# Softplus steps, second norm, attention copies and jobs of the heads placed in other slots of a hand-ordered hybrid block

## The reference

```python
xn = (x - mu) * rsqrt(var + 1e-05) * ln_g + ln_b
dt_in, Bs, Cs = split(xn @ w_xproj)                    # 64, 64, 64 columns
delta = softplus(dt_in @ w_dt + b_dt)
h = exp(dt[:, :, None] * A) * h + (dt * xt)[:, :, None] * bt[:, None, :]   # for each token, h is 128 x 64
y = einsum('bdn,bn->bd', h, ct)
ssm_out = (y + x * D_ssm) @ w_ssm_out
attn = softmax(q k / sqrt(8) + bias, window of 96 keys for each 32 queries)   # 16 heads, 4 key heads
conv_out = silu(conv4(x) + b_conv)
mem_out = x @ w_wm + b_wm + 0.3 * softmax(x dec^T / sqrt(128)) @ dec
x1 = x0 + x + 0.2*attn @ wo + 0.45*ssm_out + 0.15*conv_out + 0.2*mem_out
out = x1 + layernorm(x1) @ int4(w) + bias + (layernorm(x1) @ a) @ b
```

## Time and profile before

| what | us |
|---|---|
| median of three runs | 1112.58 (1109.39 to 1113.99) |
| the profiled execution | 1114.23 |
| its span, first to last instruction | 1112.4 |
| busy in the span: DVE, POOL, ACT, PE | 979.3, 955.6, 837.5, 830.9 |
| front, until the first scan has ended | 39.9 |
| batch 0, from there to its last scan | 136.2 |
| batches 1 to 6, between their last scans | 132.1, 129.3, 133.4, 131.0, 132.1, 129.2 |
| batch 7 | 123.1 |
| after the last scan | 26.0 |

### The profile page before, as it was taken

How to read it: one execution, slowest core, us unless ns; L and a number is a source line. 1 busy time by engine, 2 the same in 40 slices (tenths; PEclk the granted TensorE clock), 3 DMA queues, 4 the chain that set the end, 5 groups by cost and what they waited for, 6 DMA issues and landing times. The chain is left out here.

```text
span 1112.4 us, 19145 instructions
## 1 busy us (share of the span) xinstructions
PE 830.9 (75%) x4151; PEld 339.3 (30%) x4151; DVE 979.3 (88%) x2299; ACT 837.5 (75%) x2255; POOL 955.6 (86%) x675
## 2 busy tenths in 40 slices
PE   5367878688777786877778777867868778677775
PEld 2023333233323332333323333323332333232332
DVE  2688999979997999979999699897999799999991
ACT  4468886788778878687877887679887887858871
POOL 6369988989898988988899898899989898979892
PEclk9556998978997989979898798888899798989897
DMA  5845667647675666666676476665666566766630
GB/s 111 196 126 169 180 159 185 171 138 198 163 183 155 185 167 159 172 157 172 168 203 161 128 191 162 167 173 159 177 176 183 153 187 165 188 161 164 196 95 9
DMA packets 124391, 181.18 MB, mean 163 GB/s; under 512 B 29263, under 2 KB 41056, under 8 KB 124256
## 3 DMA queue, kind: packets, MB, share of 16 engines
q1 hardware_dynamic: 123968, 179.56, 61.4%
q10 hardware_dynamic: 288, 0.20, 0.1%
HBM read 170.79 MB, written 5.05 MB: 158 GB/s over the span
## 5 line engine op out<-in xcount | busy, mean ns | idle before, releaser
L1389 POOL TENSOR_TENSOR prod<-hst,C 128x1024 f32<-128x1024 f32 x256 | 602.0, 2354 | 94.9 <-DVE hst L1201 94.4
L1201 DVE TENSOR_TENSOR_SCAN hst<-decay,bank 128x512 f32<-128x512 f32 x384 | 459.5, 1209 | 3.0 <-DVE cv_a L1236 2.8
L1189 DVE TENSOR_TENSOR bank<-bank,B 128x512 f32<-128x512 f32 x384 | 263.1, 685 | 52.6 <-PE bank L911 34.8
L665 ACT ACTIVATE decay<-wide,A_rep 128x512 f32<-128x512 f32 x384 | 273.4, 715 | 41.5 <-DVE hst L1201 31.2
L911 PE MATMUL bank<-spread,sel_bc 96*128 96x512 bf16 x384 | 164.5, 434 | 101.0 <-DVE hst L1201 90.6
L679 ACT ACTIVATE prob<-s_sb,nmax 128x96 f32<-128x96 f32 x512 | 185.2, 365 | 0.9 <-DVE nmax L1214 0.5
L1405 POOL TENSOR_TENSOR uwide<-uwide,B 128x512 f32<-128x512 f32 x128 | 162.7, 1271 | 22.5 <-DMA uwide<-u_rows 22.5
L935 PE MATMUL bank<-prod,sel_red 128*32 128x512 f32 x1024 | 164.9, 722 | 0.0
L1201 DVE TENSOR_TENSOR_SCAN hst<-bank,uwide 128x512 f32<-128x512 f32 x128 | 155.4, 1214 | 2.7 <-POOL uwide L1405 2.7
L951 PE MATMUL bank<-ident,prob 128*96 128x128 f32 x512 | 85.9, 295 | 77.5 <-ACT ao L695 58.3
L944 PE MATMUL bank<-k,q 128*128 128x384 f32 x256 | 126.7, 580 | 22.3 <-DVE nmax L1214 22.2
(11 more groups left out here) (189 smaller groups left out, 1027.4 us busy)
## 6 DMA issues: line engine op xcount, KB each, us to landing
wide<-dt_rows SPq DMA_DIRECT2D x512, 256.0 KB, 4.7
uwide<-u_rows SPq DMA_DIRECT2D x128, 256.0 KB, 4.1
spread<-parts SPq DMA_DIRECT2D x66, 32.0 KB, 4.1
x_sb<-in_L_attn_x_dram SPq DMA_DIRECT2D x8, 256.0 KB, 4.5
dt_rows<-sp_t SPq DMA_DIRECT2D x8, 256.0 KB, 2.6
out_dram<-outb SPq DMA_DIRECT2D x8, 256.0 KB, 3.9
vw<-v_tok SPq DMA_DIRECT2D x80, 16.0 KB, 3.3
u_rows<-uv SPq DMA_DIRECT2D x8, 64.0 KB, 2.4
```

The costliest lines, as they stand in the source:

```text
L665: nc.scalar.activation(to, wide[m % SLOTS][:, s % 2, :], ACT.Exp, scale=A_rep[:, g:g + 1]).then_inc(exp_done, 1)
L1189: v.tensor_tensor(uP[s % 4][:, :], uP[s % 4][:, :], B2[p][:, :], ALU.mult).then_inc(dbx_done, 1)
L1201: v.tensor_tensor_scan(hst[:, s % 8, :], kept, into[:, :], 0.0, ALU.mult, ALU.add).then_inc(scan_done, 1)
L1389: g.tensor_tensor(prod[:, 2 * (m % 4):2 * (m % 4) + 2, :], hst[:, 2 * (m % 4):2 * (m % 4) + 2, :], C2[p][:, :].unsqueeze(1).to_broadcast([ ...
```

## The change

Nothing is added to or taken from the arithmetic; steps change their slot, their place in a stream or, in the front, their engine.

1. **Softplus spread.** Exp moves from slot 20 to 24, adding 1 to slot 25 (`sum`), subtracting 1 to slot 26 (`less`), Ln from 21 to 28; POOL's four steps from 22-25 to 29-32, high, r, mid, lo from 28, 30, 33, 35 to 35, 37, 39, 41. SP's stores and part DMAs follow.
2. **Second norm.** residual, aggr2, root2, normalise2: 14, 16, 17, 20 to 16, 18, 19, 23. `zT` 23 to 26, `ffn` 25/26 to 28/29, output 29 to 31. `project` starts in slot 2, not 1.
3. **Jobs.** `B` and `C` from 34, 35 to 24, 25; xaT to v two slots later; `q` 60 to 59; `es0` 30 to 33, `conv` 40 to 38, `pt0` 37 to 46, `pt2`, `pt3` 57, 59 to 56, 57, `es1`, `es3` one slot earlier.
4. **Attention copy.** `ao_copy` of block k moves from the end of slot 6+3k+11 to the next slot, right behind `unit_exp`.
5. **Front.** DVE adds and subtracts 1 in one instruction beside ACT's Ln, which no longer waits for it; SP stores dt without waiting for u, and u after the first widening; ACT makes the first two exponentials ahead of the query copies, and the key copies in slot 1.
6. **Tail.** `proj` steps of the last batch in slots 58 to 61, six and seven ahead of the last reduction and eight and nine behind it; the bias matmul of the last `ffn` goes to the scores' free bank `sP` ahead of `zT`.

```diff
-JOB_AT = {13: ("t", "back"), 15: ("p", "xaT"), 17: ("p", "xnT"), 19: ("p", "dtpre"), 21: ("p", "v"),
-          23: ("t", "zT"), 26: ("t", "ffn"), 30: ("m", "es0"), 34: ("p", "B"), 35: ("p", "C"), 37: ("m", "pt0"),
+JOB_AT = {15: ("t", "back"), 17: ("p", "xaT"), 19: ("p", "xnT"), 21: ("p", "dtpre"), 23: ("p", "v"),
+          24: ("p", "B"), 25: ("p", "C"), 26: ("t", "zT"), 29: ("t", "ffn"), 33: ("m", "es0"),
...
-LAST_PROJECT = {60: (0, 1), 61: (2, 3), 62: (4, 5), 63: (6, 7)}
+LAST_PROJECT = {58: (0,), 59: (1,), 60: (2, 3), 61: (4, 5)}
...
-BIAS_LAG, EXP_LAG, INV_LAG, NORM_LAG, PT_LAG, PT_COPY_LAG, PV_LAG, AO_COPY_LAG = 2, (3, 4), 6, 5, 9, 9, 11, 11
+BIAS_LAG, EXP_LAG, INV_LAG, NORM_LAG, PT_LAG, PT_COPY_LAG, PV_LAG, AO_COPY_LAG = 2, (3, 4), 6, 5, 9, 9, 11, 12
...
             def softplus_exp(B):
                 wait(act, sp_step, B * N_SP + SP["relu"])
                 nc.scalar.activation(sp_e[:, :], sp_e[:, :], ACT.Exp, scale=-1.0).then_inc(sp_step, 1)
+
+            def softplus_sum(B):
                 wait(act, sp_step, B * N_SP + SP["exp"])
...
-                wait(act, sp_step, B * N_SP + SP["less"])
+                wait(act, sp_step, B * N_SP + SP["exp" if first(B) else "less"])
...
             def tail(B, p):
-                for n in range(8, N_PROJ - 1):
-                    project(B, p, n)
+                project(B, p, 6)
+                project(B, p, 7)
                 reduce_group(B, GROUPS - 1)
+                project(B, p, 8)
+                project(B, p, 9)
                 project(B, p, N_PROJ - 1)
                 tail_job("back", B, p)
+                wait(pe, s_max, NB * NBLK)
+                ffn_bias(sP)
                 tail_job("zT", B, p)
-                ffn_begin(B)
-                tail_job("ffn", B, p)
+                wait(pe, done["t"], job_count("t", B, "zT"))
+                ffn_half(0, sP)
+                filled(ffn_half(1, sP), "t", B, "ffn")
...
+                dve.wait_ge(sp_step, SP["exp"])
+                v.tensor_scalar(sp_t[:, :], sp_e[:, :], 1.0, 1.0, ALU.add, ALU.subtract).then_inc(sp_step, 2)
```

More of the change, by code:

```diff
@@ L648, in front @@
                             spread_parts(act, B, p, part)
+                        for s in range(AHEAD):
+                            unit_exp(B, s)
                         act.wait_ge(const_ready, 3)
                         act.wait_ge(head_tables, 3)
-                    if name == "k":
-                        for s in range(AHEAD):
-                            unit_exp(B, s)
-                    pre_job(name, B, p, front=True)
+                    if name != "k":
+                        pre_job(name, B, p, front=True)
             def unit_exp(B, s):
@@ L757, in body @@
                         unit_exp(B + 1, s + AHEAD - UNITS)
+                    k = block_at(s, AO_COPY_LAG)
+                    if k is not None:
+                        ao_copy(B, k)
                     if first(B):
+                        if s == 1:
+                            pre_job("k", B, p, front=True)
                         setup_step(s - SETUP_AT)
@@ L773, in body @@
                         probT_copy(B, k)
-                    k = block_at(s, AO_COPY_LAG)
-                    if k is not None:
-                        ao_copy(B, k)
                     t = memory_tile_at(s, M_EXP_LAG)
@@ L796, in body @@
                             softplus_exp(B + 1)
+                        if s == AT["sum"]:
+                            softplus_sum(B + 1)
+                        if s == AT["less"]:
+                            softplus_less(B + 1)
                         if s == AT["softplus_logs"]:
@@ L834, in setup_step @@
                     pe.wait_ge(w_in, 16 * N_W_DMA)
-                    wait(pe, done["p"], job_count("p", 0, "v"))
+                    wait(pe, done["p"], job_count("p", 0, "k"))
                     transposes([epi[:, c, :] for c in range(4)], CD, 128).then_inc(init, 1)
@@ L1004, in project, with ffn_half @@
                     filled(ins, "t", B, "proj")
-            def ffn_half(h):
+            def ffn_half(h, job=jobP):
                 for t in (2 * h, 2 * h + 1):
-                    ins = mm(jobP[:, t * D:(t + 1) * D], zT[:, t * 128:(t + 1) * 128], W2[:, :], start=False, stop=True,
+                    ins = mm(job[:, t * D:(t + 1) * D], zT[:, t * 128:(t + 1) * 128], W2[:, :], start=False, stop=True,
                              skip_group_check=True)
@@ L1014, in ffn_begin, with ffn_bias @@
                 fill("t", B, "ffn")
-                mm(jobP[:, :], ones_row[:, :], bias_row[:, :].unsqueeze(1).to_broadcast([1, NT, D]), start=True, stop=False,
+                ffn_bias(jobP)
+                ffn_half(0)
+            def ffn_bias(job):
+                mm(job[:, :], ones_row[:, :], bias_row[:, :].unsqueeze(1).to_broadcast([1, NT, D]), start=True, stop=False,
                    skip_group_check=True)
-                ffn_half(0)
             def tail_job(name, B, p):
@@ L1260, in output @@
                 wait_job(dve, "t", B, "ffn")
[L1261 removed]
+                v.tensor_tensor(outb[:, :, :], (sP if last(B) else jobP)[:, :].rearrange("p (t d) -> p t d", t=NT), x1[:, :, :], ALU.add) \
                     .then_inc(out_ready, 1)
```

32 lines of the change are left out of this document (18 added, 14 removed), and 4 rows, old and new, of the table JOB_AT.

## The result

The changed kernel takes 1164.47 us (median of 4 runs, 1159.72 to 1168.39), the kernel before 1112.65 beside it (4 runs). The ratio is 1.0468, 95% interval 1.0423 to 1.0514. The forecast was 1070, with a range up to 1094: the wrong side. The profiled execution took 1159.72 us, its span 1157.9 against 1112.4.

The account below looks back on a forecast made before the run. DVE bounds the kernel, about 120 us of a 131.0 us batch, so only its idle time can be won: 35 (six middle batches) + 3.8 + 1.3 + 3.7 = 43.8 off 1114.2, forecast 1070, range 1056 to 1094.

Parts of the forecast that it names:

- the sum: DVE's idle time per middle batch after the change: 2.4 + 2.0 + 0.5 + 0.4 = 5.3 us, against 11.1 before.
- ACT's burst: Slots 23 to 28, softplus and second norm on ACT: 16.6 us of work, leaving DVE 2.0 us idle a batch.
- The walk through ACT's slots: Slots 23 to 28: ACT behind by 2.1 to 4.3 us, 6.8 after Ln; DVE stalls about 1.0 at slot 29.
- Middle batches, POOL: POOL's softplus steps moved behind slot 28: its lateness mostly costs nothing, 0.4 us of DVE idle a batch (0 to 3).
- The sum for POOL's lateness: Slot by slot against an unstalled DVE, POOL is 3.6 to 6.0 us behind from slot 31 to 43.
- The rival that POOL takes over: POOL's lateness reaches DVE through reduction and normalisation, slots 33 to 47: 3.5 us a batch, 1091 us; chance 0.12.
- Seam and slot 28: Per middle batch, the gap of about 1.0 us between batches goes to 0; DVE's wait at slot 28 falls from 1.5 to 0.5.
- the rise to 0.8: Sign to look for: PE's granted clock over slots 23 to 30 goes above 0.8, from an average of 0.70.
- Batch 0: First batch, without second norm and zT: of waits of 3.8 and 0.5 us about 0.5 stay, gain 3.8.
- Front: Before the first scan: DVE's replacement, some 0.7 us, lies beside load and Ln; gain 1.3 us (0.5 to 2.5).
- Tail: PE's chain at the end: attention steps behind the last reduction 1.6, bias matmul off the chain 2.07; gain 3.7 us (2.1 to 4.5).
- PE at its lower clock through the row of jobs: Rival: PE stays at 1.2 GHz in slots 23 to 29, DVE stalls 10 us a batch, 1125 us; chance 0.04.

Follow-up runs that it names:

- the last experiment: Changed kernel with ao_copy at its old place, high, r, mid, lo at 37, 39, 43, 45, and Ln in slot 29: 1080.65 us, ratio 0.9697.

## Why the prediction was wrong, step by step

**The step that failed** is one sentence on the middle batches: the `ao_copy` behind `unit_exp` "costs nothing on time: PE has u and scores ahead of the transposes, 0.4 + 0.9, and ACT needs 0.61 + 0.16. If ACT is late, it is late anyway." Its price was 46 to 53 us. Three things were wrong in it. It counted the exponential and the copy, but not what the slot before puts ahead of both: job copies, steps of the memory read-out, softplus steps. It took ACT's lateness as given, while these steps are exactly those that themselves wait, for PE's jobs or for POOL, so that the copy now waits for PE and PE for the copy. And the trace of the kernel before said so: the largest of PE's waits but for the one on DVE, 45.3 us in the six batches, was for `ao`, so an edit that could only lengthen this wait should have been priced from that row.

**A second step failed too**, at half that price: ACT's wait for POOL's parts of u had no term in the sum (below, 25 us). Only with both put right does the kernel come into the stated range, at 1092.5 and 1085.5.

**The 94 us between forecast and result** come apart by the experiments, by the medians and in this order: 53 for the copy (1164 to 1111), 25 for the parts of u that ACT awaited (to 1085.5), 5, likely, for Ln ahead of a copy (to 1081), and some 11 that stay open.

**Middle batches, ACT's burst.** I kept 2.0 of idle time for it. The mechanism was right: the spread is worth 3.0 to 3.5 us a batch (2.0 to 3.2 by the ratios), and with the copy back the wait for the attention exponentials is 2.8 in six batches, under the 4 I had named. In the changed kernel it is 14.0, and the copy's place alone makes the difference. The walk through ACT's slots left out what the trace shows at slot 30: with Ln in slot 28, the copy of slot 29 came late and PE's transposes waited 15.9 us for it in six batches, against 1.1 before. Exp and the additions do stand apart, as said. (The prediction gives the old burst "3.7 us of slots"; slots 20 to 22 are three, 5.6 us. The sum doesn't use that figure.)

**Middle batches, POOL.** I put 0.4 there, and looked for it in reductions and normalisations. PE's wait for POOL's products is 3.6 us in the six batches, so those did stay covered. POOL's lateness came in by another door, which had no term in the sum: ACT, in order, waits for u ahead of the high part and for r ahead of mid. The sum for POOL's lateness, 3.6 to 6.0 us in slots 31 to 43, was there; high at slot 35 is three slots behind u at 32, or 5.6 us, too little for it. Moving high, mid and lo took 25 us with the copy back and 28 with it late. The rival that POOL takes over, 21 us by way of the reduction, had the size and not the path.

**Seam and slot 28.** The waits at the seam, slots 1 and 2 of the next batch, were 6.1 us in the six batches and are 4.3, two waits of some 2 us whose releaser the profile doesn't show; with the copy back they are 4.0. That is 0.7 a batch, not under 0.3. Another 2.0 a batch came up at the scan of unit 63, which the sum had at 0, since `q` stood ahead of the copy; with the copy back it is gone. The wait that the prediction has at slot 28 stands at slot 29, by the count of scans, and its other two both at slot 24; the sum doesn't change by that. At slot 29 DVE now waits 11.3 us in the six batches for PE behind its scores (1.9 a batch, 0.5 forecast, 1.5 before), and as much with the copy back; with Ln in slot 29 it is 8.1. The granted clock of 641 to 664 is 0.79, but this stretch lies three to four slots later in its batch than that of the earlier trace rows. Over slots 23 to 30 of batch 4 the clock was 0.72 before (615.1 to 639.6) and is 0.75 (635.7 to 656.3), so the rise to 0.8 isn't there in this batch; in the mean of the six batches it is, 0.75 before and 0.87.

**Second norm and memory read-out** had 0 in the sum. DVE's waits in them are 12.1, and 13.6 + 8.0, with the copy late; 5.1, and 8.8 + 12.0, with it back, where 41 us were missing; 3.8, and 1.9 + 1.0, in the last experiment.

**Batch 0**: 3.8 faster forecast, 6.1 slower measured; 1.9 slower with the copy back (138.1), 1.2 faster in the last experiment (135.0). The old wait isn't among its waits any more; in the changed kernel 3.8 for scan exponentials, 2.4 for u and 1.8 for the convolution's gate took its place.

**Front**: 1.3 forecast, 1.1 in this pair of traces for the first scan. That is partly luck. In the twelve traces with the new front the first scan ends at 38.8 to 39.6, in the mean 39.2; in the two with the old one at 39.9 and 39.6. So the front is worth about 0.5, the low end of the range. DVE's replacement took 1.92, not 0.7. Most of it lies beside ACT's table load and Ln, but two of the steps behind it took 1.07 each, where before they took 1.19 and 0.69, and u was ready 0.8 earlier, not 1.3. The rows that answer to the earlier trace rows:

```profile
19.32 1.28 ACT L632 ACT_TABLE_LOAD   x1
19.41 1.92 DVE L1203 TENSOR_SCALAR sp_t<-xn 128x512 f32<-128x512 f32 x1 [6.21 <-ACT xn L619]
20.61 0.63 ACT L632 ACTIVATE sp_l<-xn 128x512 f32<-128x512 f32 x1
...
21.36 1.07 DVE L332 TENSOR_TENSOR sp_t<-sp_t,xn 128x512 f32<-128x512 f32 x1
22.46 1.07 DVE L332 TENSOR_TENSOR sp_l<-sp_l,sp_t 128x512 f32<-128x512 f32 x1
23.57 0.69 DVE L332 TENSOR_TENSOR sp_t<-sp_l,xa 128x512 f32<-128x512 f32 x1
...
35.57 0.70 DVE L1215 TENSOR_TENSOR bank<-bank,B 128x512 f32<-128x512 f32 x1 [7.81 <-PE bank L927]
```

**Tail**: 3.7 forecast, 4.6 measured (26.0 to 21.4), the same 21.4 with the copy late or back. The chain answers to the earlier trace rows: two attention steps ahead of the last reduction and two behind it, and no bias matmul ahead of the last ones.

```profile
1137.49 1.91 PE bank L1016 x4
1139.40 0.99 PE bank L951 x8
1140.40 1.92 PE bank L1016 x4
```

Batch 7 was put at 0; with the copy late it lost 6.3, with it back it took 122.8 against 123.1.

**The rivals** priced PE at its lower clock through the row of jobs at 1125, and gave it 0.04. The clock did fall in the mean of batches 1 to 6, from 0.89 to 0.87, and with the copy back it is 0.89 again, so it follows the copy's place; and the new waits stood outside the seven slots. The mechanism that decided stood in the text, at cost 0, and so in none of the chances.

## What to carry to other kernels

On an engine that works in order, a copy that frees a buffer for another engine costs what stands ahead of it, waits included: before moving it, list every instruction between the old place and the new one, and for each what it waits for; where that is the engine that waits for the copy, the two take turns. An edit that lengthens one of the largest waits in the trace can't be priced at nothing, even when the engine with the wait isn't the one that bounds the kernel. When a step is late behind another engine, look at who stands in order behind the waiting instruction, not only at the consumer of its data, and undo parts one at a time: here one line of a change cost 46 to 53 us and hid that the others together made the kernel a little faster (ratio 0.9942, of which front and tail are some 5 us).
